# Attention over chunks of keys in unrolled slots, with row-sum reciprocals carried by small DMAs

## Time and profile before

| what | value |
|---|---|
| median of the 3 runs | 2489.44 us |
| span of the profiled execution | 2490.1 us |
| runs' lowest and highest | 2487.39 and 2490.7 us |
| PE busy over the span | 2331.3 us (94%) |
| DVE busy | 1035.1 us (42%) |
| ACT busy | 732.1 us (29%) |
| POOL busy | 347.4 us (14%) |
| attention stage, to the experts' first matmul | 858.42 us |
| mean granted TensorE clock | 0.966 |

### The profile page before, as it was taken

The page is one execution under the profiler, slowest core; times in us unless marked ns, Lnnn a source line. Parts: engine busy times, 40 slices in busy tenths (PEclk is TensorE's granted clock), DMA queues, the critical chain, the costliest instruction groups (busy, mean ns, idle before and its releaser), DMA issues. The chain is left out here.

```text
span 2490.1 us, 40442 instructions
## 1 busy us (share of the span) xinstructions
PE 2331.3 (94%) x15186; PEld 1808.5 (73%) x15187; DVE 1035.1 (42%) x2107; ACT 732.1 (29%) x1212; POOL 347.4 (14%) x425
## 2 busy tenths in 40 slices
PE   3999999899989499999999999999999999999998
PEld 1444444444444398899898988988988898998997
DVE  6787776677765431231151141142142114123111
ACT  1565455445445131221040131131131113112110
POOL 2112222222211200110100010010010101001001
PEclk9999899889989699999999999999999999999999
DMA  7996756666651341241141141141142115114100
GB/s 195 298 240 130 130 124 145 125 123 130 133 121 68 137 129 26 56 132 26 21 143 36 21 142 44 24 139 47 26 127 59 22 20 157 21 31 126 22 17 10
DMA packets 112646, 231.83 MB, mean 93 GB/s; under 512 B 13216, under 2 KB 13216, under 8 KB 112544
## 3 DMA queue, kind: packets, MB, share of 16 engines
q1 hardware_dynamic: 85536, 174.78, 27.6%
q0 software_dynamic: 16640, 34.10, 7.8%
q10 hardware_dynamic: 10368, 21.63, 3.0%
HBM read 113.93 MB, written 68.29 MB: 73 GB/s over the span
## 5 line engine op out<-in xcount | busy, mean ns | idle before, releaser
L1035 PE MATMUL ps_h<-xhi,w1hi 128*128 128x256 f32 x2240 | 637.5, 285 | 22.4 <-DVE xlo L914 12.2
L1037 PE MATMUL ps_h<-xhi,w1lo 128*128 128x256 f32 x2240 | 639.4, 285 | 0.0
L1036 PE MATMUL ps_h<-xlo,w1hi 128*128 128x256 f32 x2240 | 636.4, 284 | 0.0
L873 ACT ACTIVATE hhi<-ps_h 128x512 fp32r<-128x512 f32 x280 | 167.1, 597 | 1161.7 <-PE ps_h L1037 1161.6
L1035 PEld LDWEIGHTS ps_h<-xhi,w1hi 128*128 128x128 f32 x2240 | 427.3, 191 | 26.0 <-issue 22.5
L1036 PEld LDWEIGHTS ps_h<-xlo,w1hi 128*128 128x128 f32 x2240 | 426.5, 190 | 1.1
L1050 PE MATMUL ps_y<-w2hi,hhi 128*128 128x512 f32 x1072 | 426.1, 397 | 0.0
L1037 PEld LDWEIGHTS ps_h<-xhi,w1lo 128*128 128x128 f32 x2240 | 425.8, 190 | 0.0
L1052 PE MATMUL ps_y<-w2hi,hlo 128*128 128x512 f32 x1072 | 423.4, 395 | 0.0
L1051 PE MATMUL ps_y<-w2lo,hhi 128*128 128x512 f32 x1072 | 423.3, 395 | 0.0
L946 DVE SCALAR_TENSOR_TENSOR hlo<-ps_h,hhi 128x512 fp32r<-128x512 f32 x280 | 193.6, 691 | 519.0 <-ACT hhi L873 519.0
(11 more groups left out here) (119 smaller groups left out, 1822.4 us busy)
## 6 DMA issues: line engine op xcount, KB each, us to landing
raw<-in_L_ffn_w SPq DMA_DIRECT2D x128, 512.0 KB, 4.7
dispatched<-xrow ACTq DMA_DIRECT2D x8, 2640.0 KB, 17.6
xin<-dispatched SPq DMA_DIRECT2D x40, 528.0 KB, 3.7
qst<-qhi SPq DMA_DIRECT2D x64, 256.0 KB, 6.8
kst<-khi SPq DMA_DIRECT2D x64, 256.0 KB, 10.3
xt<-in_x SPq DMA_DIRECT2D x32, 256.0 KB, 4.6
ct<-in_ctx SPq DMA_DIRECT2D x32, 256.0 KB, 4.5
kst<-klo SPq DMA_DIRECT2D x32, 256.0 KB, 8.6
```

What stands on the lines that cost most here:

```text
L873: nc.scalar.activation(hhi[:, 2 * f:2 * f + 2, :], ps_h[f % 4][:], ACT.Relu).then_inc(hhi_ready, 1)
L1035: nc.tensor.matmul(to, w1hi[:, c, fs], xhi[:, c, :], start=(c == 0), stop=False)
L1036: nc.tensor.matmul(to, w1hi[:, c, fs], xlo[:, c, :], start=False, stop=False)
L1037: last = nc.tensor.matmul(to, w1lo[:, c, fs], xhi[:, c, :], start=False, stop=(c == NC4 - 1))
```

## The change

It rewrites the attention stage; the experts' stage stays as it is.

- All slots are unrolled, -3 to 37 (`SLOTS` = G + 6), with constants in place of loop registers.
- In a slot the outer step is a chunk c and the inner one i. The scores of head c and queries i are made with the transposed scores of head i and keys c, so after a chunk the four heads' probabilities for these keys are complete.
- One narrow visit follows each chunk: 8 instructions into `ps_o` and 8 into `ps_l` at once (`weighted`). `probs` becomes three buffers of one chunk each.
- `ps_a` and `ps_b` go. `ps_s` and `ps_t` are rings of 3 banks each, which the small uses share; the turn of each is worked out ahead (`bank_turns`).
- Row sums: ACT copies `ps_l`, SP moves 4 rows of 512 to 64 rows of 32 (`l_wide`), DVE takes reciprocals there and splits them (`r_hl`), SP moves them back with two DMAs as 8 rows (`r_rows`), and PE spreads them with one matmul of 128 by 512 (`to_dims`). Runs are of 32 elements. The transposes of `l_sb` and the 16 matmuls with `linv` go.
- x1 (the residual addition) moves from DVE to POOL. POOL no longer waits for its scatters before its next slot; `xrow` is a ring of 6, and the landing is awaited two pairs later.
- The zero fill is 10 DMAs of 2.16 MB, one in each of slots 1, 2, 3, 4, 6, 7, 8, 9, 11, 12; each covers a slice of every expert, and the pairs wait on the slices they need.
- At the start the loads come first, constants are made in slots -1 and 0, and the selection rows go to `kst` by 4 DMAs instead of 4 DVE copies. `xrow` work is done one slot earlier (lag 4), the pairs at 6 and 7 slots instead of 8 and 9.

```diff
-U = 8
+SLOTS = G + 6
+RING = 6
+FILLS = CAP // P
+LW = 16
...
-        probs = [sb(f"probs{i}", [P, HPG, NC4, D]) for i in range(2)]
-        sel = probs[0][:, 0]
+        probs = [sb(f"probs{i}", [P, HPG, D]) for i in range(3)]
+        sel = probs[2]
...
-        ps_s = [... for i in range(2)]
-        ps_t = [... for i in range(2)]
+        ps_s = [... for i in range(3)]
+        ps_t = [... for i in range(3)]
-        ps_a = stack.enter_context(nc.psum_tensor("ps_a", [P, D], F32))
-        ps_b = stack.enter_context(nc.psum_tensor("ps_b", [P, D], F32))
...
 SP
+            for s in range(-3, SLOTS):
+                if live(s - 3):
+                    g = s - 3
+                    sp.wait_ge(l_saved, g + 1)
+                    if g >= 2:
+                        sp.wait_ge(r_whole, g - 1)
+                    sp.dma_start(l_wide[g % 2][:], l_sb[g % 2][0:P:HD, :].rearrange("h (c q) -> h c q", c=LW)
+                                 ).then_inc(l_ld[g % 2], 16)
...
+                if live(s - 3):
+                    g = s - 3
+                    sp.wait_ge(r_ready, g + 1)
+                    if g >= 2:
+                        sp.wait_ge(s_done, s_turn["r", g - 2])
+                    for part in range(2):
+                        sp.dma_start(r_rows[g % 2][HPG * part:HPG * part + HPG, :].bitcast(F32
+                                     ).rearrange("h (c q) -> h c q", c=LW),
+                                     r_hl[g % 2][:, part, :].bitcast(F32)).then_inc(r_ld[g % 2], 16)
...
 POOL
-                    for half in range(2):
-                        pool.wait_ge(row_st[s.ring(9 - half, 8)], s.rounds(9 - half, 8) * (16 * TOPK))
+                if live(s - 3):
+                    g = s - 3
+                    pool.wait_ge(s_free, s_turn["r", g])
+                    pool.wait_ge(res_ld[g % 4], 16 * turns(g, 4))
+                    if g >= 2:
+                        pool.wait_ge(x1_st[g % 2], 16 * turns(g - 2, 2))
+                        pool.wait_ge(x2_ready, g - 1)
+                    nc.gpsimd.tensor_tensor(x1[g % 2][:], o_sb[g % 2][:], xres[g % 4][:], ALU.add
+                                            ).then_inc(x1_ready, 1)
...
 ACT
+                for n in range(FILLS):
+                    if s == 1 + 5 * n // 4:
+                        act.dma_start(disp_rows[n], fill[:].unsqueeze(1).to_broadcast([P, E, ROW])
+                                      ).then_inc(fill_st[n // 2], 16)
...
 DVE
+                        if (c, i) == (1, 2) and live(s - 3):
+                            g = s - 3
+                            dve.wait_ge(l_ld[g % 2], 16 * turns(g, 2))
+                            nc.vector.reciprocal(r_wide[:], l_wide[g % 2][:]).then_inc(r_whole, 1)
+                            dve.wait_ge(r_whole, g + 1)
+                            nc.vector.tensor_copy(r_hl[g % 2][:, 0, :], r_wide[:]).then_inc(r_hi, 1)
+                            dve.wait_ge(r_hi, g + 1)
+                            nc.vector.tensor_tensor(r_hl[g % 2][:, 1, :], r_wide[:], r_hl[g % 2][:, 0, :].bitcast(F32),
+                                                    ALU.subtract).then_inc(r_ready, 1)
...
+                        if (c, i) == (2, 3) and live(s - 3):
+                            dve.wait_ge(s_done, k)
+                            dve.wait_ge(o_saved, g + 1)
+                            nc.vector.tensor_tensor(o_sb[g % 2][:], ps_s[(k - 1) % 3][:], o_sb[g % 2][:], ALU.mult
+                                                    ).then_inc(s_free, 1)
...
 PE
+            def weighted(g, c):
+                n = 4 * g + c
+                pe.wait_ge(t_free, t_turn["t", g, c, HPG - 1])
+                if c == 0:
+                    pe.wait_ge(t_free, t_turn["vt", g])
+                    if g >= 1:
+                        pe.wait_ge(o_saved, g)
+                        pe.wait_ge(l_saved, g)
+                for h in range(HPG):
+                    hd = slice(HD * h, HD * h + HD)
+                    nc.tensor.matmul(ps_o[hd, :], vt[g % 4][:, c, hd], probs[n % 3][:, h, :],
+                                     start=(c == 0), stop=(c == NC4 - 1))
+                for h in range(HPG):
+                    hd = slice(HD * h, HD * h + HD)
+                    done = nc.tensor.matmul(ps_l[hd, :], ones[:, 0:HD], probs[n % 3][:, h, :],
+                                            start=(c == 0), stop=(c == NC4 - 1))
+                done.then_inc(pv_done, 1)
...
+            for s in range(SLOTS):
+                for c in range(NC4):
+                    for i in range(HPG):
+                        cols = slice(P * i, P * i + P)
+                        if live(s):
+                            bank = s_bank(s_turn["s", s, c, i])
+                            nc.tensor.matmul(bank[:], qst[s % 4][0:STACK, c, cols], kst[s % 4][0:STACK, c, :],
+                                             start=True, stop=True).then_inc(s_done, 1)
+                        if live(s - 2):
+                            g = s - 2
+                            cols = slice(P * c, P * c + P)
+                            bank = t_bank(t_turn["t", g, c, i])
+                            nc.tensor.matmul(bank[:], kst[g % 4][0:STACK + MROWS, i, cols],
+                                             qst[g % 4][0:STACK + MROWS, i, :], start=True, stop=True).then_inc(t_done, 1)
...
+                    if c == 2 and live(s - 3):
+                        g = s - 3
+                        pe.wait_ge(r_ld[g % 2], 32 * turns(g, 2))
+                        bank = s_bank(s_turn["r", g])
+                        nc.tensor.matmul(bank[:], to_dims[:], r_rows[g % 2][:], start=True, stop=True).then_inc(s_done, 1)
+
+                    if c == 0 and live(s - 3):
+                        weighted(s - 3, NC4 - 1)
+                    if c > 0 and live(s - 2):
+                        weighted(s - 2, c - 1)
```

More of the change, by code:

```diff
@@ L45 @@
 NRAW = 4
[L48 to L82, removed]
@@ L130, in attention_and_dispatch @@
         counted = sb("counted", [P, E])
+        fill = sb("fill", [P, ROW])
         xt = [sb(f"xt{i}", [P, D]) for i in range(4)]
@@ L149, in attention_and_dispatch @@
         mrow = sb("mrow", [HD, D], F32R)
-        o_sb = sb("o_sb", [P, D])
-        l_sb = sb("l_sb", [P, D])
-        linv = [sb(f"linv{i}", [P, NC4, HPG]) for i in range(2)]
+        o_sb = [sb(f"o_sb{i}", [P, D]) for i in range(2)]
+        l_sb = [sb(f"l_sb{i}", [P, D]) for i in range(2)]
+        l_wide = [sb(f"l_wide{i}", [HPG * LW, D // LW]) for i in range(2)]
+        r_wide = sb("r_wide", [HPG * LW, D // LW])
+        r_hl = [sb(f"r_hl{i}", [HPG * LW, 2, D // LW], F32R) for i in range(2)]
+        r_rows = [sb(f"r_rows{i}", [MROWS, D], F32R) for i in range(2)]
+        to_dims = sb("to_dims", [MROWS, P], F32R)
+        dims = sb("dims", [HPG, P])
         x1 = [sb(f"x1_{i}", [P, D]) for i in range(2)]
         st2 = [sb(f"st2_{i}", [P, 12]) for i in range(2)]
-        xrow = [sb(f"xrow{i}", [P, ROW]) for i in range(8)]
+        xrow = [sb(f"xrow{i}", [P, ROW]) for i in range(RING)]
         x2t = sb("x2t", [P, D])
-        fill = xrow[7]
         lg = [sb(f"lg{i}", [P, 2, E]) for i in range(2)]
@@ L392, in _ @@
         @block.vector
         def _(dve):
-            nc.vector.memset(sel[:], 0.0).then_inc(dve_const, 1)
-            for i in range(2):
-                nc.vector.memset(nmax_hl[i][:], 0.0)
-            for i in range(7):
-                nc.vector.memset(xrow[i][:, IDCOL:ROW], 0.0)
-            nc.vector.memset(counted[:], 0.0)
-            nc.vector.memset(fill[:], 0.0).then_inc(dve_const, 1)
-            dve.wait_ge(dve_const, 2)
-            nc.vector.memset(fill[:, IDCOL:IDCOL + 1].bitcast(I32), S).then_inc(dve_const, 1)
@@ new lines, in q_stats, with q_var @@
+            def q_stats(g):
+                dve.wait_ge(x_ld[g % 4], 16 * turns(g, 4))
+                if g >= 2:
+                    dve.wait_ge(rs1, g - 1)
+                nc.vector.bn_stats(st1[g % 2][:, 0:6], xt[g % 4][:]).then_inc(stat1, 1)
+            def q_var(g):
+                dve.wait_ge(stat1, g + 1)
+                nc.vector.bn_aggr(st1[g % 2][:, 6:8], st1[g % 2][:, 0:6]).then_inc(var1, 1)
+                dve.wait_ge(var1, g + 1)
+                nc.vector.tensor_scalar(st1[g % 2][:, 8:9], st1[g % 2][:, 7:8], EPS, None, ALU.add).then_inc(veps1, 1)
@@ L559, in _ @@
[L559 to L568 removed]
+                        if (c, i) == (2, 1) and live(s + 2):
+                            q_scaled(s + 2)
@@ new lines, in _, with layer @@
+            pe.wait_ge(rt["counted"], B)
+            bank = s_bank(s_turn["total"])
+            nc.tensor.matmul(bank[:, 0:E], ones[:], counted[:], start=True, stop=True).then_inc(s_done, 1)
+def layer(nc, x, ctx, klen, wg, w1, w2, out, disp):
+    x_rows = x.rearrange("b c l -> (b c) l")
+    ctx_rows = ctx.rearrange("b c l -> (b c) l")
+    out_rows = out.rearrange("b c l -> (b c) l")
+    with nc.sbuf_tensor("totals", [P, E], I32) as totals:
```

(2 more changed lines are left out.)

746 lines of the change are left out of this document (385 added, 361 removed).

## The result

The changed kernel takes 2595.87 us (median of 4 runs, 2591.91 to 2598.06) against 2488.41 (2484.31 to 2490.7) for the kernel before on the same chip: ratio 1.0433, 95% interval 1.0416 to 1.0449. It is 107 us slower where I had forecast 108 us faster.

The account below looks back on a forecast made before the run. PE was taken to bound the attention stage; a slot of 18.3 us work, 1.2 wait and 0.9 dips makes 20.4 instead of 25.15. With start and drain this gave -107.5 us, from 2490.1 to 2382 us, range 2305 to 2455.

Parts of the forecast that it names:

- What bounds the kernel before: Attention stage: PE bounds it; waits, mainly from POOL awaiting its scatters, and clock dips add 4.7 us a slot.
- PE's own work, 18.3 us: Attention slot: 20.7 us less 1.3 for four merged visits and 1.15 for reciprocals' work leaves PE 18.3 us.
- Start: Before the first scores: loads first and constants off the path bring them from 33.47 to 21 us, -12.5.
- POOL's landing wait gone: In the slots, POOL no longer waits for its scatters (`dispatched`), and the waits at L684 go with it.
- the hop: Each small transfer of the row sums' round trip: 2.5 us to land, between nothing and 3.7.
- DVE "in line" at nothing: DVE's three small operations on the row sums: 0.6 us in line, nothing counted for DVE by itself.
- the dip: PE's clock after a 1.2 us wait: 1.7 us lost in every second slot, counted as 0.9 a slot.
- Sum: Whole kernel: slot of 20.4 us; start, slots and drain together -107.5 us from 2490.1, giving 2382 us.
- the drain: From the logits of slot 31 to the experts' first matmul, 82.35 us before: -11 us (-25 to 0).
- The zero fill: Slots 3 to 12: slower small hops under the fill add 2.5 us, making 22.9 us a slot.
- The rival "slower": PE's wait after c = 2: hops of 5 us behind copies and scatters, 25.1 us a slot, 2502 us; chance 0.07.
- rival "round trip or DVE": Attention slot: hops of 3.7 us, or DVE waiting in line, make 22.5 us a slot, 2426 us; chance 0.25.

Follow-up runs that it names:

- Experiment 4: Kernel before, with POOL's wait for the landing of its scatters moved behind the next pair's scatters in three of four pairs: 2432.54 us, ratio 0.978.
- experiment 2: Changed kernel without the row sums' round trip, a constant 0.05 in `r_rows`, so the experts' routing differs: 2335.64 us, ratio 0.9391 to the kernel before.
- experiment 5: Changed kernel with DVE's three reciprocal operations four reductions later and what follows them moved too: 2378.83 us, ratio 0.9557 to the kernel before.
- experiment 1: Changed kernel with only the transfer into `l_wide` moved from SP's to ACT's queue: 2643.62 us, ratio 1.0628 to the kernel before.

## Why the prediction was wrong, and where it was right

- **What bounds the kernel before: right, with two thirds of its price.** Experiment 4 takes POOL's wait away and the slot falls from 25.15 to 22.0 us, 3.1 of the 4.7 I had put on the waits and their dips. PE's wait at the logits is left (10.5 us in 9 waits); whether it makes the rest wasn't tried.
- **PE's own work, 18.3 us: right as far as it was seen.** A merged visit takes 394.59 - 392.73 = 1.86 us, forecast 1.85:

```profile
392.73 1.06 PE L673 MATMUL ps_o<-probs,vt 128*32 128x512 f32 x8
393.62 1.04 PE L677 MATMUL ps_l<-probs,ones 128*32 128x512 f32 x8
394.59 0.50 PE L690 MATMUL ps_s<-kst,qst 96*128 96x512 f32 x1
```

  Without the round trip a slot is 19.7 us at the full clock. In a slot of experiment 2, PE waits at three places for 0.2 to 0.3 us, for DVE's reductions and for ACT's probabilities, about 1 us with the gaps they make; for DVE I had put nothing into the sum and 0 to 1 into the range. In experiment 5 every second slot is 18.7 us, which leaves at most 0.4 above the 18.3.
- **Start: right.** 21.80 against 21. **POOL's landing wait gone: right.**
- **The failed step: the hop, "Between nothing and the 3.7 us of a 256 KB load ... I take 2.5".** For a hop with nothing ahead of it 2.5 was right: 2.33 and at most 2.83 were measured. But no hop goes alone here. I placed the three loads ahead of `r_rows` and nothing ahead of `l_wide`. I missed that SP's copies into `kst` await PE's last transposed scores of the slot, so that 12 us of copies are issued at the slot's end, 4 to 8 us ahead of `l_wide`. The hop took 7.3 us. I had the DMA row, 14 us of transfers in a slot, and used it as an average, not to ask when in the slot they run.
- **Second failed step: DVE "in line" at nothing.** I wrote "DVE does three operations in line" and priced their 0.6 us, and then looked for the wait at PE's spreading matmul. A wait in DVE's line stops the reductions behind it, and three banks cover 3 x 0.68 = 2 us of that, 0.68 being one reduction. DVE reads the hop more than a chunk ahead of the place that I watched; once DVE had stopped for it and PE for DVE, `r_rows` was never late. My own sign of being wrong, "if PE waits mostly on DVE's reductions", is what came. Experiment 5 shows the size: with the same hop, read four reductions later together with all that follows it, 217 of the 253 us that the round trip costs are gone.
- **Third: the dip, 1.7 us in every second slot, from a 4 us stretch of before.** After a stall of 4 to 5.5 us it was some 8 us at 1.2 GHz, 4 us lost, and by the clock of the stretches in every slot.
- **Sum.** A slot is 28.2, not 20.4. At the logits of slot 31 (884.43, against a forecast of 776.07 - 96.5 = 679.6) this is 205 us; the drain gained 2.9 us, not 11, which adds 8. That is the whole 213 us between the forecast and the measured time. The drain's term was too large whatever the hop: in experiment 5 it is 747.15 - 668.65 = 78.5 us, a gain of 3.9. Why wasn't looked into.
- **The zero fill: my 2.5 us a slot was not seen apart.** From slot 4 to 9 a slot is 29.1 us and later 28.2, and DVE's wait for the hop 6.9 us (41.1 in 6 waits, from 110 to 280 us) against 5.8: the fill adds about a microsecond to what is there without it. In experiment 5 a slot is (284.70 - 112.86) / 8 = 21.5 us from slot 4 to 12 and 20.3 later, so 1.2 us, half of my term.
- **The rival "slower"** had the nearest mechanism, a hop over 4.8 us because the copies fill the queue. It got 0.07, at the wrong engine, PE, and its 2502 us stood well short. The rival "round trip or DVE" even named DVE "waiting in line for the first hop", at 22.5 us. In both, the hop was a number with a top of 3.7 or 5 us, not followed to what is issued ahead of it. The two had 0.32 together. The stated chances also miss their own parts by 0.01: these add up to faster 0.93, same 0.02, slower 0.05.
- By coincidence in part, experiment 5 stands at 2379 us, where I had put the kernel after: its slot of 20.3 has next to no wait of DVE, one of PE for `r_rows` of 1.6 us in about every second slot, and a clock of 0.98, close to the slot that I had described.

The fixed 2.0 us that the Trainium skill gives a transfer ("DMA: Bandwidth & Descriptors", "Anatomy of one DMA") is fitted there to transfers that GpSimd issues; the 2.33 us of a hop from SP's queue with free engines agrees with it. The hop behind a backlog took three times that. The same page's "Specifications" warn of runs under 512 B; the 128 B runs here show no price that can be seen in 2.33 us.

What stays open: why experiment 1 is 48 us slower than the kernel after. DVE's wait for the hop is 7.6 us there (98.5 in 13) against 5.8; that a load goes ahead of the hop fits the trace, but wasn't tried by itself. Nor was any one of the moves that experiment 5 makes together, nor the unrolling.

## What to carry to other kernels

Before an engine is made to wait in line for a small transfer, list what is issued ahead of it and when in the period it is issued: an average DMA share hides a burst, and a lone landing time is no estimate behind one. Put the wait as late in the engine's line as its consumers allow, and price it by what is queued behind it on that engine, not only by the consumer at the end of the chain. A stall of TensorE of 4 to 5.5 us counts nearly double here, so an operation moved by a few places can be worth more than the work that a change saves.

## What I had not expected of the hardware

- Issuing the small transfer from another engine's queue didn't shorten it: 8.2 us on ACT's own queue, with one load more ahead of it, 7.3 on SP's. Order of issue did: 2.3 to 2.8 us with the copies behind it.
- The stack copies within SBUF, 256 KB into 32 partitions each, run at about 130 GB/s with the DMA share at 1.09; loads with a similar share run at 248. Six of them are 12 us, so a slot's copies cost as much engine time as twice their bytes in loads.
- After a stall of 5.5 us, PE was granted the lower clock for some 8 us, though it was busy all that time; in the kernel before, after shorter waits, the dips were about 4 us.
